# Attention scores as pairs of 64-row tiles in two PSUM banks, and another planner limit for ScalarE and VectorE

## The reference

```python
scores = jnp.einsum('blhd,bmhd->bhlm', q, k) * scale        # self-attention, causal mask, then softmax
attn = jax.nn.softmax(scores, axis=-1)                      # and the same for both cross-attentions, 77 keys
...
def step(h, xt):
    h_new = jnp.tanh(xt + h @ Wh.T + bh)                    # 1024 steps, one after the other
    return (h_new, h_new)
```

## Time and profile before

| what | value |
|---|---|
| time, median of 3 runs | 1327.06 us (1326.94 to 1333.12) |
| profiled execution | 1336.98 us, span of its instructions 1335.2 us |
| PE busy | 1291.6 us (97%), 19651 matmuls |
| VectorE (DVE) busy | 857.7 us (64%) |
| ScalarE (ACT) busy | 626.6 us (47%) |
| GpSimd busy | 88.5 us (7%) |
| mean granted clock of TensorE | 0.968 of full speed |

### The profile page before, as it was taken

One profiled execution on the slowest core, in us unless ns is written; L12 is line 12 of the kernel. 1 busy time (PEld: TensorE's weight loads), 2 busy tenths in 40 slices (PEclk: granted clock), 3 DMA queues, 4 the chain that ended last, 5 costly groups with the idle time before them and its releaser, 6 DMA issues.

```text
span 1335.2 us, 48515 instructions
## 1 busy us (share of the span) xinstructions
PE 1291.6 (97%) x19651; PEld 894.3 (67%) x19651; DVE 857.7 (64%) x2733; ACT 626.6 (47%) x2842; POOL 88.5 (7%) x156
## 2 busy tenths in 40 slices
PE   5799999999999999999999999999999999999998
PEld 3465446777766777776677777766767677766555
DVE  7875587268777228787843257667755754566486
ACT  2163313844434783543467866543344455433322
POOL 2110100001000000100000010100000000000100
PEclk9799789999999999999999999979999999989999
DMA  6544300001000001100000023100000100001100
GB/s 192 123 124 149 65 1 2 22 15 44 3 3 5 13 9 41 42 3 3 2 27 3 4 99 108 39 3 2 2 2 19 50 3 3 18 2 35 32 1 17
DMA packets 52288, 44.48 MB, mean 33 GB/s; under 512 B 12203, under 2 KB 51302, under 8 KB 52070
## 3 DMA queue, kind: packets, MB, share of 16 engines
q1 hardware_dynamic: 47398, 40.39, 10.4%
q10 hardware_dynamic: 1600, 0.79, 0.3%
q0 software_dynamic: 3072, 0.21, 0.1%
HBM read 25.81 MB, written 15.15 MB: 31 GB/s over the span
## 4 chain that ended last, share of the span: by engine, by line
PE 92%; DVE 4%; DMA 1%; issue 1%; ACT 1%; SPq 0%; DVEq 0%; ACTq 0%
PE b L532 23%; PE b L1708 10%; PE b L1478 7%; PE b L1072 6%; PE b L549 6%; PE b L1043 5%; PE b L1778 5%; PE b L983 5%; PE b L714 4%; PE b L1336 3%; PE b L1311 3%; PE b L762 2%; PE b L473 2%; PE b L63 2%; PE b L666 2%; PE b L518 2%
## 5 line engine op out<-in xcount | busy, mean ns | idle before, releaser
L532 PEld LDWEIGHTS b<-hp,whp 128*128 128x128 f16 x12276 | 476.6, 96 | 244.1 <-ACT hp L575 160.6
L532 PE MATMUL b<-hp,whp 128*128 128x2 f16 x12276 | 533.2, 165 | 1.4 <-DVE hp L581 0.5
L581 DVE TENSOR_TENSOR hp<-hist,hp 128x4 f16<-128x4 f32 x1023 | 165.0, 161 | 340.8 <-ACT hist L576 328.1
L575 ACT ACTIVATE hp<-b 128x4 f16<-128x4 f32 x1024 | 177.6, 173 | 433.1 <-PE b L532 422.5
L992 DVE TENSOR_REDUCE mx<-b 128x1 f32<-128x512 f32 (+3 forms) x304 | 194.0, 654 | 2.5 <-PE b L986 1.7
L1057 ACT ACTIVATE vp<-b 128x512 f32<-128x512 f32 x288 | 170.9, 604 | 40.5 <-PE b L1046 26.6
L576 ACT ACTIVATE hist<-b 128x4 f32<-128x4 f32 x1024 | 178.9, 175 | 0.0
L1708 PE MATMUL b<-vp,heads 128*128 128x512 f16 x576 | 167.6, 386 | 0.0
L983 PE MATMUL b<-heads 128*128 128x512 f16 (+3 forms) x384 | 112.0, 335 | 5.5 <-DVE mx L992 3.4
L549 PE MATMUL b<-whp 128*128 128x512 f16 (+7 forms) x431 | 112.3, 332 | 0.0
L1478 PE MATMUL b<-we,xT 128*128 128x512 f16 x384 | 111.5, 383 | 0.0
(11 more groups left out here) (236 smaller groups left out, 1654.0 us busy)
## 6 DMA issues: line engine op xcount, KB each, us to landing
x_qs<-qx_scr SPq DMA_DIRECT2D x64, 96.0 KB
qx_scr<-xq_pair SPq DMA_DIRECT2D x16, 256.0 KB, 2.1
heads<-q_scr SPq DMA_DIRECT2D x32, 96.0 KB
heads<-k_scr SPq DMA_DIRECT2D x12, 192.0 KB, 4.7
x<-in_x SPq DMA_DIRECT2D x8, 256.0 KB, 6.7
q_scr<-tail SPq DMA_DIRECT2D x8, 256.0 KB, 2.3
k_scr<-tail SPq DMA_DIRECT2D x8, 256.0 KB, 2.3
x_qs<-in_L_ffn_We SPq DMA_DIRECT2D x2, 1024.0 KB, 5.6
```

The source lines that it names most:

```text
L532: return pe.matmul(self.z(t)[:, m], self.w.whp[:, a, k, m * P:(m + 1) * P], self.g.hp16[:, (t - 1) % 2, part, k, :], start=False, stop=Tru ...
L575: act.activation(self.g.hp16[:, t % 2, 0], self.z(t), ACT.Tanh, scale=1 / LIFT).then_inc(self.s["hi_ready"], 1)
```

## The change

Score matmuls of an even and an odd head now read only their own 64 rows (`rows_of`), one right after the other, and write to two banks. A piece of such work takes both banks at once (`rooms` in the planner lets an operation open several) and has one signal at its end, for which the readers of both banks wait. Masks are added behind all the products of a piece. Items with one key tile, and blocks on the end of the diagonal, stay as they were, in full rows and one bank. Banks now hold heads of one parity, so the reductions and exponentials write every other head. The planner adds SWITCH = 0.1 us to the cost of a pair. In the first pass a piece may be planned when all but FIRST_PAIRS = 1 of the reductions of the items before it are (before: all but FIRST_BANKS − 1 = 2).

Besides, the planner's limit for other work on ScalarE and VectorE is 0.15 us while fewer than 768 tanhs are planned; it stays 0.3 on the other engines.

```diff
+LATE_ON = {"act": 0.15, "v": 0.15}
...
+        def rooms(k):
+
+            keys = k.opens(k.next) if k.opens else None
+            return [] if keys is None else keys if isinstance(keys, list) else [keys]
...
-                    if k.opens and k.opens(k.next) is not None:
-                        if not idle:
-                            continue
-                        at = max(at, min(idle, key=lambda b: b[0])[0])
+                    banks = len(rooms(k))
+                    if banks > len(idle):
+                        continue
+                    if banks:
+                        at = max(at, sorted(b[0] for b in idle)[banks - 1])
...
-                        late = self.late if by_name["tanh"].next < HURRY else HURRIED
+                        late = LATE_ON.get(e, self.late) if by_name["tanh"].next < HURRY else HURRIED
...
+SWITCH = 0.1
+FIRST_PAIRS = 1
...
+def rows_of(h):
+
+    return slice(64 * (h % 2), 64 * (h % 2) + 64)
...
-                self.items += [(j, h, 1, 4 * full, 4) for h in range(H)]
-            if rest:
-                step = 4 // rest
-                self.items += [(j, h, step, n - rest, rest) for h in range(0, H, step)]
+                self.items += [(j, h, h + 1, 4 * full, 4) for h in range(H)]
+            if rest == 3:
+                self.items += [(j, h, h + 1, n - rest, rest) for h in range(H)]
+            if rest == 2:
+                self.items += [(j, HG * hg + p, HG * hg + HG, n - rest, rest) for hg in range(NG) for p in range(2)]
+            if rest == 1:
+                self.items += [(j, h, h + HG, n - rest, rest) for h in range(0, H, HG)]
...
+        self.pieces = []
+        for i, item in enumerate(self.items):
+            if item[4] > 1 and item[1] % 2:
+                self.pieces[-1].append(i)
+            else:
+                self.pieces.append([i])
...
-            self.score_items += [(n, 0, HG, P)] if last else [(n, 0, 2, 0), (n, 2, 2, 0)]
+            self.score_items += [(n, 0, 1, P)] if last else [(n, 0, 2, 0), (n, 1, 2, 0)]
...
+               opens=lambda n: [("self_first", i) for i in self.pieces[n]],
+               behind=[("self_highest", lambda n: self.pieces[n][0] - FIRST_PAIRS)])
...
+        return heads * (0.0535 * n_tiles + 0.01) + masks + SWITCH * (len(self.pieces[n]) > 1)
...
+        for e in range(len(self.heads_in(piece[0]))):
+            for i, o in zip(piece, banks):
+                h = self.heads_in(i)[e]
+                rows = rows_of(h) if len(piece) > 1 else slice(0, P)
+                last = pe.matmul(o[:, N * e:N * e + N], self.qs[rows, H // 2 * (h % 2) + h // 2, column(j):column(j) + P],
+                                 self.ks[rows, b, h // 2, P * first:P * first + N], start=e == 0, stop=not diagonal,
+                                 skip_group_check=True)
+        if diagonal:
+            for i, o in zip(piece, banks):
+                for e in range(len(self.heads_in(i))):
+                    last = pe.matmul(o[:, N * e + N - P:N * e + N], self.g.identb[:], self.g.mask_qk[:], start=False,
+                                     stop=True, skip_group_check=True)
...
+        return (HG * 0.064 if first else 2 * 0.117 + SWITCH) + 0.06 * HG * (kb >= 2 * self.units[u][0])
...
+        for e in range(HG):
+            h, at, o = HG * hg + e, N * (e // step), banks[e % step]
+            rows = rows_of(h) if step > 1 else slice(0, P)
+            last = pe.matmul(o[:, at:at + N], self.ks[rows, b, h // 2, P * kb:P * kb + P],
+                             self.qs[rows, H // 2 * (h % 2) + h // 2, QW * b + first:QW * b + QW], start=e < step,
+                             stop=not diagonal, skip_group_check=True)
...
-        act.wait_ge(self.s["s2"], i + 1)
+        act.wait_ge(self.s["s2"], n + 1)
...
-        st.add("pe", name + "_scores", self.scores, 2 * len(self.units), 0.23, lambda i: of_unit(i // 2) + 0.3,
-               opens=lambda i: (name + "s", i), behind=[(name + "_values", lambda i: i // 2 - 1)])
+        st.add("pe", name + "_scores", self.scores, len(self.units), 0.23 + SWITCH, lambda u: of_unit(u) + 0.3,
+               opens=lambda u: [(name + "s", 2 * u + p) for p in range(2)],
+               behind=[(name + "_values", lambda u: u - 1)])
...
+        for e in range(HG):
+            h, at = HG * hg + e, QW * (e // 2)
+            rows = rows_of(h)
+            last = pe.matmul(banks[e % 2][0:M2, at:at + QW], ks[rows, b, h, :], self.qs[rows, h // 2, QW * b:QW * b + QW],
                              start=True, stop=True)
```

More of the change, by code:

```diff
@@ L978, in first_pass @@
             pe.wait_ge(self.g.shaped, MASK_QK)
-        for e in range(heads):
-            h = head + e
-            at = P * n * e
-            diagonal = self.is_diagonal(i)
-            last = pe.matmul(o[:, at:at + P * n], self.qs[:, H // 2 * (h % 2) + h // 2, column(j):column(j) + P],
-                             self.ks[:, b, h // 2, P * first:P * first + P * n], start=True, stop=not diagonal)
-            if diagonal:
-                last = pe.matmul(o[:, at + P * n - P:at + P * n], self.g.identb[:], self.g.mask_qk[:], start=False, stop=True)
+        diagonal, N = self.is_diagonal(piece[0]), P * tiles
@@ L1243, in load_q @@
         if n:
-            sp.wait_ge(self.s["s2"], 2 * B * (g - NG + 1))
+            sp.wait_ge(self.s["s2"], B * (g - NG + 1))
         pairs = slice(HG // 2 * hg, HG // 2 * hg + HG // 2)
```

94 lines of the change are left out of this document (48 added, 46 removed).

## The result

| what | before | after |
|---|---|---|
| time, median of 3 runs | 1327.06 us | 1387.10 us (1381.32 to 1390.43) |
| ratio | | 1.040, 95% interval 1.035 to 1.046 |
| profiled execution | 1336.98 us, span 1335.2 | 1390.43 us, span 1388.7 |
| ahead of the first tanh | 204.7 us | 208.8 us |
| the recurrence, first to last tanh | 1010.7 us | 1052.7 us |

Slower by 4.0%, where 1.4% faster was forecast and 1342 us was the end of the range. Of the 53.5 us that the span grew, 42 lie in the recurrence.

A forecast was written before the change was run, and what follows sets the result against it. It took TensorE's time, loosely packed, as the bound. Terms of −13, −7 and +2 gave −18 us against the profiled 1336.98; scaled to the median of 1327.06 that is 1309 us, 1.4% faster, range 1285 to 1342.

The forecast's parts named there:

- Part one: Score matmuls as pairs of row tiles: 304 pieces each 0.05 us shorter, 15 us, less 2 kept by slots.
- Part two: Lower limit for other work on ScalarE and VectorE before step 768: fewer late tanhs, at most 15 us, minus 7 taken.
- Part three: Two banks and one signal a piece: readers wait longer, bounds 0 to 38 us, plus 2 us taken.
- Cheap switch: Entering and leaving row tiles costs 0.1 us or is hidden by the slot: 1291 us, chance 0.15.
- Weights of the second pair wait: In four-head pieces, weight loads into still streaming rows can't go ahead: 208 pieces pay 0.097 us more, 1329 us, chance 0.10.
- Freed time becomes filler: The chain keeps the shorter slots and deferred work returns as lateness; 3 us stay: 1324 us, chance 0.10.
- VectorE becomes the bound: In dense first passes, lower limit leaves VectorE too little room; about 250 steps 0.15 us longer: 1346 us, chance 0.18.
- No overlap: Row tiles don't run beside each other; 336 pieces pay 0.16 us more and save nothing: 1376 us, chance 0.05.
- Pairs 0.11 apart, 0.09 behind: Sign in a piece of four 256s that its price is right: 0.11 us pair to pair, 0.09 before, 0.2 behind.
- Fewer late tanhs: Sign on ScalarE: fewer tanhs start 0.2 us late; if the 99 stay, the lower limit's forecast is wrong.
- L549 well over 130 us: Sign in TensorE's fillers: near 112 us expected; well over 130 speaks for filler or VectorE as the rival.
- a recurrence of 1010 us or more: Sign that the whole prediction is wrong: first to last tanh still takes 1010 us or more.

## Why the prediction was wrong

**The sum.** The prediction had −13 −7 +2 = −18 us. In points of the time before, with the experiments taken in one order, the pieces in full rows bring +3.5 (1.035), the limit on top of them −1.7 (1.018) and the tiles on top of both +2.2 (1.040); with the limit first it is +2.0 by itself (1.020), −0.2 for the pieces and the same +2.2. Slower had a chance of 0.25, but through rivals that are not what happened for the most part; no term, rival or sign dealt with TensorE's clock, and 1387 lies beyond the worst of them, 1376.

**What bounds the kernel.** "So the limit is TensorE's time, loosely packed" holds, and the rest of the argument did not keep to it. I then counted lateness of steps as time saved. With ScalarE's limit the recurrence lost 24.6 us and the span only 10.6; with both limits it reached step 740 39 us sooner and waited 52.6 us. Less lateness is less time only if TensorE's other work still finds room and the first layer still arrives.

**Part one, minus 13.** The price of a piece was right: 0.22 + 0.09 + 0.06 for four 256s, where 0.38 was forecast. What failed is the step from there to the sum, "304 pieces by 0.05 are 15 us". It took TensorE's clock as given. In the same order the tiles changed the time by +2.2 points, some +30 us, instead of minus 13, while the clock fell from 0.977 to 0.917. The Trainium skill, TensorE: Matmul & The Clock Gate, Part 1, says that the gate follows how busy TensorE has been. The traces show more than the busy row can: PE is busy for 50.0 of 50 us with the clock at 0.50 and for 49.9 with it at 1.00, in the same order, and only the rows that the scores use differ.

**Part two, minus 7.** The sign of the direct effect was right: of the 99 tanhs that were over 0.15 us late 49 are left (worked out the same way), and all lateness of this kind fell from 22.7 to 14.1 us. The net of part two was wrong in sign by itself, +2.0% (1.020), and right on top of the pieces in full rows (1.018 for 1.035); the prediction has one term for both and didn't ask where the recurrence meets its supply. I had written "from below it is a loss, since what may not start starts a step later" and then took half the gain; the loss was the larger part.

**Part three, plus 2.** This is the term that was mis-sized most, some 47 us for 2 by itself. Pieces of two banks in full rows with the old limit cost 3.5%, of which about one point is that the planner was told less than full rows take. My bounds were 0 to 38 us for the wait of the readers; I took 2, "near the lower end". That wait is the smaller part, as far as ScalarE's tanhs show it: in this kernel they start some 10 us later in all behind their finished products than before. I take the rest to be that a piece of 0.4 us can't be divided: where it doesn't fit in front of the next step, the planner holds it back and fills the slot, or the recurrence goes short while the first layer runs 105 us ahead. No run has pieces of two banks and one signal that are small, so this is argued. The fillers, 176.9 us for 112.3, speak for the first; how the loss divides between the two stays open. Limit and pieces balance each other in part: the one delays the first layer, the other the recurrence, so that with both in full rows (1.018) the time is under that with pieces alone.

**The rivals.** *Cheap switch*: no, 0.09 behind a piece stays. *Weights of the second pair wait*: no; four 256s take 0.23 us to the next tile piece. The Trainium skill's rule in TensorE: Matmul & The Clock Gate, Part 3, that loads overlap only with matmuls of other row groups, would have made it 0.33 by the 0.097 of a load; the trace disagrees. Nor did its 3.07 times for four tiles, spread evenly, carry over to two: a pair starts within 4 ns and takes half the time (0.22 us streamed for 0.43). *Freed time becomes filler*: the mechanism was there, and it made 37 us of filler instead of eating 15. *VectorE becomes the bound*: right in sign and in the engine (its limit alone costs 1.0%), wrong in its place. I looked for longer steps from 500 to 650 us, where 150 steps were done for 147 before; what happened is that the reductions ended 30 us later and the bill came at step 740. *No overlap*: refuted by the 0.33 against 0.54 us.

**The signs I had named.** Pairs 0.11 apart, 0.09 behind: seen. Fewer late tanhs: seen, and no proof of a gain. L549 well over 130 us: seen, 148.9. The sign for being wrong altogether, a recurrence of 1010 us or more: it took 1052.7.

## What to carry to other kernels

Price a denser form of a matmul with TensorE's clock in the sum: here one that uses half the rows cost more clock than columns, so look at the row PEclk of a first trial before you count what it saves. In a kernel whose order is planned around a chain, list the points where the chain meets its supply and how long before its use each input is ready; work that is held back for the chain is paid there or behind the chain's end. And try the larger pieces by themselves first: here they cost 3.5% in full rows, where the best that the overlap promised was 1%.

## What the hardware showed that I had not expected

- With score matmuls on 64 of 128 rows the granted clock was lower: in one and the same order 0.977 in full rows, 0.917 as pairs of row tiles, 0.802 on the same 64 rows one after the other. In another order 0.988 in full rows and 0.884 in tiles.
- The half clock lasted for 96 us on end while the page has PE busy for all of it; it came in stretches of second-pass and cross pieces between value products on column tiles (32 columns), and did not with the first pass's tiles alone. Second-pass tiles between value products also ran at full clock, from 450 to 500 us of the same execution, and executions of one kernel with tiles lay between clocks of 0.874 and 0.953. What starts such a stretch, and whether the column tiles are needed for it, stays open.
- Two full-row matmuls of 128 columns behind each piece brought that stretch back to full clock (1.00 for 0.50) and cost more than it gave, 1.051 in all.
- Row tiles cost 0.09 us when full rows follow (0.33 for four 256s that stream 0.22 in pairs), and nothing that can be seen from one tile piece to another of different work (0.23).
